# Attention with DMA for the small transposes, an earlier read of sums and maxima, and a fused scale and gate in the mix

## The reference

```python
y = _ln_cf(y, out_norm_w, out_norm_b)          # (y - mean) / std * w + b, over channels
y = y * silu(z)                                # the gate
x = x + einsum('cd,bdhw->bchw', out_proj_w, y)
```

```python
theta, phi, g = conv1x1(x, ...), conv1x1(x, ...), conv1x1(x, ...)   # each 96 x 4096
p = softmax(einsum('bon,bom->bnm', theta, phi), axis=-1)            # 4096 x 4096
y = einsum('bnm,bom->bon', p, g)
out = conv1x1(y, W_w, W_b) + x
```

## Time and profile before

| | us |
|---|---|
| median of 3 runs | 10093.42 |
| fastest and slowest of them | 10088.11, 10101.04 |
| profiled execution, its own time | 10092.67 |
| span of the profiled execution | 10090.8 |
| one image (a stage pattern that comes eight times) | 1276 - 662 = 614 us from mix to end of attention |

### The profile page before, as it was taken

One profiled execution on the slowest core, in us unless ns is written; L12 is line 12 of the kernel. 1 busy time (PEld: TensorE's weight loads), 2 busy tenths in 40 slices (PEclk: granted clock), 3 DMA queues, 4 the chain that ended last, 5 costly groups with the idle time before them and its releaser, 6 DMA issues.

```text
span 10090.8 us, 108759 instructions
## 1 busy us (share of the span) xinstructions
PE 9260.9 (92%) x28420; PEld 4969.4 (49%) x28420; DVE 7541.6 (75%) x8593; ACT 6270.0 (62%) x7748; POOL 3449.7 (34%) x1937
## 2 busy tenths in 40 slices
PE   7999989999899998999979999899998999989999
PEld 3336733367333663336633366333663336633366
DVE  6976669766697666976669766697667976679766
ACT  6755667556675556755567555675556755567555
POOL 3850038400484004840048400484004840048400
PEclk9999989999899998999999999899998999999999
DMA  1320013200131001310013100131001310013100
GB/s 57 110 67 7 8 56 107 63 8 6 56 107 63 8 6 56 107 63 8 6 56 108 62 8 6 61 108 57 8 6 62 107 57 8 7 62 107 57 8 8
DMA packets 159892, 488.46 MB, mean 48 GB/s; under 512 B 21721, under 2 KB 22713, under 8 KB 126606
## 3 DMA queue, kind: packets, MB, share of 16 engines
q1 hardware_dynamic: 159374, 482.72, 15.1%
HBM read 455.38 MB, written 27.26 MB: 48 GB/s over the span
## 4 chain that ended last, share of the span: by engine, by line
PE 66%; DVE 14%; issue 13%; ACT 3%; POOL 2%; DVEq 1%; SPq 0%; ACTq 0%; POOLq 0%; DMA 0%
DVE h L1088 7%; PE ps L546 5%; PE ps L559 5%; PE ps L547 5%; PE ps L548 5%; PE ps L561 5%; PE ps L560 5%; PE ps L469 4%; PE ps L430 3%; PE ps L392 2%; PE ps L427 2%; PE ps L384 2%; PE ps L411 2%; PE ps L414 2%; PE ps L328 2%
## 5 line engine op out<-in xcount | busy, mean ns | idle before, releaser
L1213 DVE TENSOR_TENSOR pl<-pf,ph 128x1024 fp32r<-128x1024 f32 x1024 | 1254.7, 1225 | 1215.5 <-ACT ph L868 1214.4
L1088 DVE TENSOR_TENSOR_SCAN h<-ps,h,dbu 128x512 f32<-128x512 f32 x1536 | 1884.5, 1268 | 18.7 <-DVE h L1114 5.3
L942 POOL TENSOR_TENSOR dbu<-bs,du 128x1024 f32<-128x1024 f32 x768 | 1799.0, 2372 | 52.8 <-POOL du L933 52.8
L868 ACT ACTIVATE ph<-pf 128x1024 fp32r<-128x1024 f32 x1024 | 1085.3, 1060 | 830.7 <-PE ps L561 830.4
L888 POOL MEMSET sqb<- 64x512 f32 x16 | 8.3, 519 | 4271.9 <-issue 4267.0
L860 ACT ACTIVATE pf<-ps 128x1024 f32<-128x1024 f32 x1024 | 1051.1, 1026 | 651.4 <-PE ps L548 651.4
L742 ACT ACTIVATE ps<-dt,negA 128x512 f32<-128x512 f32 x1536 | 1033.0, 684 | 439.7 <-DVE h L1088 404.8
L1197 DVE TENSOR_REDUCE mx<-ps 128x1 f32<-128x512 f32 x1792 | 1165.1, 684 | 69.3 <-PE ps L469 41.8
L1096 DVE TENSOR_TENSOR hc<-h,ps 128x1024 f32<-128x1024 f32 x768 | 937.9, 1221 | 190.8 <-PE ps L403 110.4
L933 POOL TENSOR_TENSOR du<-dt,u 128x512 f32<-128x512 f32 x512 | 706.7, 1402 | 623.4 <-DVE dt L1078 623.4
L559 PE MATMUL ps<-ph,gth 128*97 128x512 f32 x2048 | 817.1, 399 | 80.8 <-ACT yraw L848 72.1
(11 more groups left out here) (188 smaller groups left out, 16077.4 us busy)
## 6 DMA issues: line engine op xcount, KB each, us to landing
bs<-rows SPq DMA_DIRECT2D x256, 1024.0 KB, 5.2
bs<-rows SPq DMA_DIRECT2D x512, 256.0 KB, 6.1
xa<-in_x SPq DMA_DIRECT2D x130, 256.0 KB, 2.9
xb<-in_x SPq DMA_DIRECT2D x130, 128.0 KB, 3.0
out<-fa SPq DMA_DIRECT2D x64, 256.0 KB, 2.0
out<-fa SPq DMA_DIRECT2D x64, 128.0 KB, 2.3
rows<-xd SPq DMA_DIRECT2D x256, 8.0 KB
gate<-in_sel SPq DMA_DIRECT2D x1, 384.0 KB
```

The source lines that it names most:

```text
L868: A(ph[:, mp % 2, :, :], pf[:, mp % 2, :, :], ACT.Copy).then_inc(S["ph_ready"], 1)
L942: pool.tensor_tensor(dbu[:, q, :, :], bs[par][:, q, :, :], du[:, r:r + 1, :].to_broadcast([P, 2, T]), ALU.mult).then_inc(S["dbu_ready"], 1)
L1088: dve.tensor_tensor_scan(h[:, j, ::step], ps[:, 2 + e, ::step], dbu[:, q, e, ::step], h[:, j, end:end + 1], ALU.mult, ALU.add)\
L1213: TT(pl[:, mp % 2, :, :], pf[:, mp % 2, :, :], ph[:, mp % 2, :, :].bitcast(F32), ALU.subtract)\
```

## The change

Three things are changed.

- The row of softmax sums goes to columns by a DMA (`dcol`), VectorE takes the reciprocal (`invert`), a DMA writes it to DRAM (`rden`), and another reads it back as a row on 96 partitions (`rdb`), which `divide` uses. The negated maxima (`nmr`) go straight into row 96 of the next `thc` by four DMAs of 128 elements. All are issued by SP, in one stream with the stores, and TensorE's first scores of a chunk wait for the four. The matmuls `turn_den`, `spread_den` and `shift` and the copy `take_shift` remain only for the first shift and the last chunk of an image.
- `read_sum` stands ahead of the exponential of place 2. The tops stand at places 1 to 12, with three from place 5 on, `negate` at place 13 instead of 14. The finishing steps move to places 5, 8, 10 and 12.
- In the mix four `scalar_tensor_tensor` operations take the place of the six: (d * weight) * rstd, and (d + bias) * gate. The first two have no wait between them.

```diff
-        TOPS = [0] + [2] * 7 + [3] * 6 + [0] * 2
+        TOPS = [0] + [2] * 4 + [3] * 8 + [0] * 3
-        DEN_AT, RB_AT, WY_AT, WR_AT = 3, 4, 7, 9
+        DEN_AT, RB_AT, WY_AT, WR_AT = 5, 8, 10, 12
...
@@ SP, in attention
+                def attend(c, par, before, nxt):
+                    i = b * NCH + c
+                    d = b * (NCH - 1) + c
+                    if before:
+                        sp.wait_ge(S["yraw_ready"], i + 1)
+                        sp.dma_start(dcol[:, :], yraw[O:O + 1, :].rearrange("o (p j) -> o p j", j=4)).then_inc(S["den_loaded"], 16)
+                        sp.wait_ge(S["rden_ready"], i)
+                        sp.dma_start(rden.rearrange("(p j) -> p j", j=4), rcol[:, :]).then_inc(S["den_saved"], 16)
+                        sp.wait_ge(S["den_saved"], d * 16)
+                        sp.dma_start(rdb[:, :], rden.unsqueeze(0).to_broadcast([O, T])).then_inc(S["rb_loaded"], 16)
+                        store(c - 1)
+                    if nxt:
+                        sp.wait_ge(S["nmx_ready"], i + 2)
+                        for t in range(4):
+                            sp.dma_start(thc[1 - par][0][O:O + 1, t * P:(t + 1) * P].bitcast(F32), nmr[:, t:t + 1].bitcast(F32))\
+                                .then_inc(S["shift_loaded"], 16)
@@ TensorE, scores
-                    if mp == 0:
-                        pe.wait_ge(S["thc_ready"], i + 1)
+                    if mp == 0 and first:
+                        pe.wait_ge(S["thc_ready"], b + 1)
+                    elif mp == 0:
+                        pe.wait_ge(S["thl_ready"], i + 1)
+                        pe.wait_ge(S["shift_loaded"], b * (64 * (NCH - 1)) + (c * 64 + 64))
@@ TensorE, attend
-                            if mp == DEN_AT:
+                            if mp == WY_AT:
                                 if nxt:
                                     pe.wait_ge(S["thf_ready"], i + 2)
-                                turn_den(i - 1)
-                            if mp == RB_AT:
-                                spread_den(i - 1)
-                            if mp == WY_AT:
                                 output(i - 1, 0)
...
-                        if nxt and mp == MP - 2:
-                            if before:
-                                pe.wait_ge(S["fin_ready"], i * 2 + 2)
-                            shift(i + 1)
@@ ScalarE, attend
-                        if mp == MP - 1 and nxt:
-                            take_shift(i + 1, 1 - par)
+                        if mp == LAG and before:
+                            read_sum(i - 1)
                         act.wait_ge(S["st_ready"], s + 1)
                         act.wait_ge(S["pl_ready"], s + 1)
                         A(pf[:, mp % 2, :, :], ps[:, 2 * (mp % 2):2 * (mp % 2) + 2, :], ACT.Exp)\
                             .then_inc(S["pf_ready"], 1)
                         if mp == 0 and nxt:
                             split_theta(i + 1, 1 - par)
-                        if mp == LAG and before:
-                            read_sum(i - 1)
@@ VectorE, mix
-                        link(TT(da[:, :], da[:, :], rstd[:, :], ALU.mult), "mix_link", at + 1)
-                        link(TT(db[:, :], db[:, :], rstd[0:R, :], ALU.mult), "mix_link", at + 2)
-                        link(TS(da[:, :], da[:, :], vecs[:, V_ONW:V_ONW + 1], vecs[:, V_ONB:V_ONB + 1],
-                                ALU.mult, ALU.add), "mix_link", at + 3)
-                        link(TS(db[:, :], db[:, :], vecs[0:R, V_ONW + 1:V_ONW + 2], vecs[0:R, V_ONB + 1:V_ONB + 2],
-                                ALU.mult, ALU.add), "mix_link", at + 4)
+                        STT(da[:, :], da[:, :], vecs[:, V_ONW:V_ONW + 1], rstd[:, :], ALU.mult, ALU.mult).then_inc(S["mix_link"], 1)
+                        STT(db[:, :], db[:, :], vecs[0:R, V_ONW + 1:V_ONW + 2], rstd[0:R, :], ALU.mult, ALU.mult)\
+                            .then_inc(S["mix_link"], 1)
                         sl = bass.ds((c + 1) * T, T)
-                        TT(oa[:, :], da[:, :], gate[:, 0, sl], ALU.mult).then_inc(S["gated_ready"], 1)
-                        TT(ob[0:R, :], db[:, :], gate[0:R, 1, sl], ALU.mult).then_inc(S["gated_ready"], 1)
+                        dve.wait_ge(S["mix_link"], at + 1)
+                        STT(oa[:, :], da[:, :], vecs[:, V_ONB:V_ONB + 1], gate[:, 0, sl], ALU.add, ALU.mult)\
+                            .then_inc(S["gated_ready"], 1)
+                        dve.wait_ge(S["mix_link"], at + 2)
+                        STT(ob[0:R, :], db[:, :], vecs[0:R, V_ONB + 1:V_ONB + 2], gate[0:R, 1, sl], ALU.add, ALU.mult)\
+                            .then_inc(S["gated_ready"], 1)
@@ VectorE, attention
-                def invert(i):
-                    dve.wait_ge(S["den_ready"], i + 1)
-                    dve.reciprocal(rcol[:, :], ps[:, 7, 0:4]).then_inc(S["inv_link"], 1)
...
+                def invert(c):
+                    dve.wait_ge(S["den_loaded"], b * (16 * (NCH - 1)) + (c * 16 + 16))
+                    dve.reciprocal(rcol[:, :], dcol[:, :]).then_inc(S["rden_ready"], 1)
+
+                def divide(c):
+                    dve.wait_ge(S["rb_loaded"], b * (16 * (NCH - 1)) + (c * 16 + 16))
+                    TT(yn[:, :], yraw[0:O, :], rdb[:, :], ALU.mult).then_inc(S["yn_ready"], 1)
```

More of the change, by code:

```diff
@@ L146, in build @@
         yraw = sb("yraw", [O + 1, T], where=aty)
+        nmr = sb("nmr", [P, 4], F32R, where=aty)
+        dcol = sb("dcol", [P, 4], where=aty)
+        rdb = sb("rdb", [O, T], where=aty)
         yn = sb("yn", [O, T], where=aty)
@@ L164, in build @@
         ps = ctx.enter_context(nc.psum_tensor("ps", [P, 8, T], F32))
+        rden = nc.dram_tensor("rden", [T], F32, kind="Internal").ap()
         rows = [nc.dram_tensor(f"rows{i}", [NS, T], F32, kind="Internal").ap() for i in range(2)]
@@ L197, in build @@
             "thc_ready", "st_ready", "pf_ready", "ph_ready", "pl_ready", "pv_ready", "yraw_ready", "den_ready", "inv_link", "rden_ready",
-            "rb_ready", "yn_ready", "wy_ready", "fin_ready", "out_stored")}
+            "rb_ready", "den_loaded", "den_saved", "rb_loaded", "shift_loaded", "yn_ready", "wy_ready", "fin_ready", "out_stored")}
         block = ctx.enter_context(nc.Block())
@@ L307, in _, with store @@
                     load((b + 1) % nb, (b * 2 + 2) * NCH + q, q, q)
-                with sp.Fori(0, NCH) as c:
+                def store(c):
                     sp.wait_ge(S["fin_ready"], (b * NCH + c) * 2 + 4)
@@ L312, in _ @@
                     sp.dma_start(outr[b, P:C, sl], fa[0:R, 1, :]).then_inc(S["out_stored"], 16)
+                def attend(c, par, before, nxt):
[14 more added lines that the diff above has]
+                                .then_inc(S["shift_loaded"], 16)
+                run_attend(sp, attend)
+                store(NCH - 1)
                 barrier(sp, b, 3)
@@ L535, in shift, with scores @@
                     q.then_inc(S["shift_ready"], 1)
-                def scores(mp, i, par):
+                def scores(mp, c, i, par, first):
                     s = i * MP + mp
-                    if mp == 0:
-                        pe.wait_ge(S["thc_ready"], i + 1)
+                    if mp == 0 and first:
[3 more added lines that the diff above has]
+                        pe.wait_ge(S["shift_loaded"], b * (64 * (NCH - 1)) + (c * 64 + 64))
                     pe.wait_ge(S["pf_ready"], s + 1)
@@ L591, in attend @@
                     for mp in range(MP):
-                        scores(mp, i, par)
+                        scores(mp, c, i, par, not before)
                         if mp == 0 and nxt:
@@ L841, in take_shift @@
                     act.wait_ge(S["thl_ready"], i + 1)
-                    act.wait_ge(S["shift_ready"], i + 1)
+                    act.wait_ge(S["shift_ready"], b + 1)
                     A(thc[par][0][O:O + 1, :], ps[O:O + 1, 7, :], ACT.Copy).then_inc(S["thc_ready"], 1)
@@ L993, in _ @@
                             ("y1_added", 1), ("rows_saved", 16), ("scan_link", 6), ("dbu_ready", 4), ("du_ready", 2), ("dtpre_ready", 1), ("phl_ready", 1), ("gtl_ready", 1),
-                            ("top_read", 2), ("pf_ready", 2), ("yraw_ready", 1), ("pv_ready", 2), ("pl_ready", 2),
+                            ("top_read", 2), ("pf_ready", 2), ("yraw_ready", 1), ("shift_loaded", 64), ("pv_ready", 2), ("pl_ready", 2),
                             ("yn_ready", 1), ("out_stored", 32)):
@@ L1198, in top, with negate @@
                         .then_inc(S["top_read"], 1)
-                def negate(i, first=False):
+                def negate(i, c, first=False):
                     dve.wait_ge(S["top_read"], i * NU + NU + 2)
@@ L1206, in negate @@
                     else:
-                        dve.wait_ge(S["shift_ready"], i)
-                        dve.tensor_reduce(nmx[:, :], mx[:, :, :], AX.X, ALU.max, negate=True)\
+                        dve.wait_ge(S["shift_loaded"], b * (64 * (NCH - 1)) + c * 64)
```

(25 more changed lines are left out.)

2 lines of the change are left out of this document (1 added, 1 removed).

## The result

The changed kernel takes 9787.97 us (median of 4 runs, 9786.11 to 9790.28), beside 10095.44 us for the kernel before: a ratio of 0.9696, with a 95% interval of 0.9679 to 0.9713. That is 307 us less, where 281 were forecast; 9788 lies inside the stated range and 2 us outside the likeliest case's own. Placed again beside three experiments it took 9796.49 us (5 runs, 9787.74 to 9799.09; ratio 0.9703, 0.969 to 0.9716).

The account below looks back on a forecast made before the run. TensorE was taken to bound attention, with VectorE and TensorE taking turns in the mix. 22.3 + 8.75 - 1.8 + 5.8 = 35.1 us an image, 281 us in eight, gave 9812 us, range 9775 to 9870.

Parts of the forecast that it names:

- likeliest case: The forecast for the whole kernel: 9790 to 9835 us, given 57%.
- Matmuls removed: Attention: three kinds of matmul leave TensorE in 7 chunks, 1.16, 1.16 and 0.87 us each; 22.3 us an image.
- The read of the sums: Attention: copying `yraw` ahead of the exponential saves 1.25 us in each of 7 chunks; 8.75 us an image.
- The middle chunk as a whole: Attention: the period of the middle chunks falls by about 4.1 us.
- `divide` in place 8: Attention: VectorE's added product makes TensorE wait about 0.3 us in 6 chunks; -1.8 us an image.
- rival of VectorE as the bound: Places with three maxima: 0.8 instead of 0.3 us lost in 48 chunks, +24 us, 9836; 8%.
- The transfers: SP's queue: seven added transfers a chunk stay hidden; the last shift transfer has 3.5 us to land, nothing lost.
- first of the rivals: Shift row comes late: tiny pieces take the mean packet's time, 1.1 us in 48 chunks, +53 us, 9865; 14%.
- The slower rival: Shift row's pieces run one after another on one engine; near 14,000 us, or 11,000 at 25 us a row; 5%.
- The mix: Four fused operations for six: 1.14 us before the first chunk, 3.7 in five later, 1.0 last; 5.8 us an image.
- fused operations' record of 0.74 us: Mix: a fused VectorE operation takes 0.74 us, as with one PSUM operand, not the projection's 0.96.
- rival of more gain: Mix gains all seven chains, 8.0 us an image, and `divide` costs nothing: 32 us more, 9780; 9%.

Follow-up runs that it names:

- shift_matmul: The changed kernel with the row of maxima made by matmuls and the ScalarE copy again, instead of the four transfers: 9849.92 us, ratio 0.9755.
- late_sum: The changed kernel with the copy of the sums put back behind the exponential of place 2: 9871.59 us, ratio 0.9774.
- old_tops: The changed kernel with the tops at their old places, so the maxima are negated one place later (14): 9847.76 us, ratio 0.9751.
- eight_dma: The changed kernel with the row of maxima in eight transfers of 64 elements instead of four of 128: 9851.44 us, ratio 0.9755.
- rb_at_six: The changed kernel with `divide` at place 6, one place behind `invert` instead of three: 9899.03 us, ratio 0.9804.
- att_only: The changed kernel with the six operations of the mix put back, so only attention is changed: 9872.7 us, ratio 0.978.

## Why the prediction was right, and where it was short

- **Matmuls removed.** Right: 448 of each kind are gone, and shift_matmul gives one of the three back at the price stated.
- **The read of the sums.** Right, 1.25 forecast and 1.30 in the middle chunks; late_sum gives it back.
- **The middle chunk as a whole.** Its period was to fall by about 4.1 us and fell by 3.91. `divide` has 0.14 of the difference; the rest was not traced. That attention comes out at 29.9 us an image for 29.3 is partly luck: six middle periods give 23.5 for 24.8, and the first and last chunks 6.4 for 4.4, a surplus that no run takes apart.
- **`divide` in place 8.** The place, the cause and the sign were right; the size was 0.44 and not 0.3 us, since the idle time was taken for the loss. The rival of VectorE as the bound (0.8 us) did not come.
- **The transfers.** Right: hidden, as the pieces' small size had suggested. The slack came out at 1.2 us where 3.5 - 2.0 = 1.5 was forecast. The first of the rivals was nearer than its chance says: old_tops or eight_dma make the row late, at 0.7 to 1.0 us of idle time where 1.1 had been priced, though by a later start or more issues and not by slow pieces. The way of the reciprocal is 5 us and not 4.1, because the read-back of 192 KB lands in 3.4 us where I took the 2.0 of a store; the slack was large enough.
- **The slower rival.** 128 pieces of 4 bytes land in 2.0 us, not in 20 (128 x 0.153) and not in the 25 estimated for a tile; a strided transfer of one vector is no transposed tile.
- **The mix.** This is the term that was mis-sized: 5.8 us an image against 8.6 measured, 22 us of the 26 by which the result is faster than forecast. The prediction's step was that in the five later chunks the gain is TensorE's idle time, 3.7 us, because then its own stream sets the pace. The mechanism holds (the waits go, but for one late by 0.3 us, and the chain's further gain is lost), and two things were missing from the sum. A wait costs 0.27 us more than its idle time, which makes 4.8 us, and 1.1 for 1.0 at the last wait; each step fell by 0.84 to 1.01 us where 0.7 was forecast. The larger one stood at nothing: the clock, about 1.6 us an image, which falls behind the idle stretch ahead of the first products with the old chain and stays up with the new. 1.05 + 4.8 + 1.1 + 1.6 = 8.6. The fused operations' record of 0.74 us, chosen over 0.96, was right; the chain came out 0.11 us shorter, for the moving address costs nothing visible. The rival of more gain (9780) came within 8 us by luck: it gave the mix 8.0 us for all seven chains and let `divide` cost nothing, neither of which is so. No fused step took the 0.78 us worked out for a wait behind each: all four take 0.66.

## What to carry to other kernels

Where TensorE is busy for 96% of a stage, price a wait from start to start of the matmuls around it, not by the idle time beside it. Small changes of layout can leave TensorE for a DMA queue when their result is wanted some 6 us later; count 0.6 us of the queue for each transfer and 2.0 us to the last landing, and then look who asks next, and what stands ahead in the queue. On an in-order engine, put the other tile's operation between a result and its reader; here that alone gave 3.6 of the mix's 8.6 us, and fusing gave the rest. When waits of TensorE grow longer, look at the granted clock behind them before adding up the idle time.

## What the runs showed of the hardware

- A wait of TensorE costs 0.26 to 0.28 us beyond its recorded idle time: in the 48 middle chunks of the changed kernel (0.18 us idle), at the 56 late rows of old_tops (0.67 to 0.77), at the 40 waits for the squares before (0.56 to 1.06) and in the 48 chunks of rb_at_six (1.59 to 2.36), in float32 pairs as in the single-pass stream. Only behind the copy of the sums it is less (1.43 lost for 1.22). 0.10 to 0.11 of it is the first matmul, followed after 0.34 us instead of 0.233 (0.53 instead of 0.43 in the pairs); 0.16 to 0.17 is that the last matmul's record (0.40 us where the step is 0.233, 0.59 where it is 0.43) ends that much behind the start that the next one could have had.
- The clock fell from 1.00 to 0.50 behind idle stretches of 1.71 us and more (rb_at_six), and stayed at 1.00 behind others of up to 3.25 us (att_only, second image); no run here separates what decides. A fall costs 1.4 to 1.7 us of TensorE.
- The landing time of a small transfer hardly depends on the size of its pieces: 2.0 us for 128 x 4 bytes and for 128 x 16 bytes within SBUF, 1.4 us for 128 x 16 bytes to DRAM.
